# New orders of the engines' tasks in a four-layer decoder stack of 32 elements

## The chip, the cores and the metric

One core of a Trainium2 chip runs the whole program. The metric is the device time of one execution in microseconds (us). A core has five engines that run side by side, each through its own list of instructions in order: TensorE (PE, matmuls), VectorE (DVE), ScalarE (ACT), GpSimd (POOL) and SyncE (SP, which issues the DMAs here). They wait for one another by semaphores.

## What is computed

For each of 32 elements (128 tokens of 256 channels, and a context of the same size) four layers run one after the other. Cut to what matters:

```python
# layer 0: attention of x to the context, 16 heads; only element 0's result is added, to all elements
x = x + att(x, ctx)[0]
# layer 1: a Mamba-2 block, then a cross-attention with 8 heads
zxbcdt = rms(x) @ in_proj_w                  # z, xBC, dt
xBC = silu(conv(xBC)); dt = softplus(dt + dt_bias)
y = scan over tokens of (decay, dt * x, B) with C; y = y + D_skip * x
x = x + rms(y * silu(z)) @ out_proj_w
x = x + softmax(q k / sqrt(dh)) v @ Wo
# layer 2: causal self-attention, attention to the context (16 heads each, keys cut at a
# length counted from nonzero energies), a feed-forward; a layer norm behind each
# layer 3: causal attention to the context, layer norm, feed-forward with gelu, sum
```

## The kernel before

The work of an element is cut into some 80 tasks with names (`Q2`, `conv0`, `quads3`, `scan` ...). A task has a part on each engine that it needs: of `Q2`, PE does a projection, ACT copies it out of PSUM (`QB`), POOL makes a product for the first query. Elements are interleaved: while the Mamba block of element n runs, the cross-attention of n-1, the two attentions of n-2 and the last layer of n-3 run beside it. `l` is the element's lane (0 to 3), `it.iteration` its group of four.

What runs when is not computed on the chip: each engine has a written-out order. `TASKS` gives a place for each task, `PERIOD` 14 is added for each element, `FIRST` moves the tasks of the first eight elements, `LAST` those of the last six, and `SETUP` places what runs once (layer 0 and the loading and preparing of weights). Sorted, this is PE's order. `SHIFT` moves tasks against it for the other engines. The numbers are places to sort by and nothing else; no instruction waits for a time. Each engine's program is then a loop over its order. For the orders the sort is all:

```python
STAND = {(task, n % G, n // G): place_of(task, n) for task in TASKS for n in range(B)} | {(task, 0, 0): at for task, at in SETUP.items()}
PLACE = {key: n for n, key in enumerate(sorted(STAND, key=STAND.get))}
ORDER = dict(PE=list(PLACE))
for engine, shift in SHIFT.items():
    ORDER[engine] = sorted(PLACE, key=lambda key: round(STAND[key] + shift.get(key[0], 0), 5))
```

From PE's order also follow which of the four PSUM banks (`ring0` to `ring3`, in turn) a task's output takes, and the turns of the four score banks. `SPARE` puts some unneeded matmuls (L634) ahead of a few tasks of the first elements, and is not changed.

The tasks that the prediction follows:
- `Y`: PE multiplies the decays with the inputs of the scan (L858). It waits for `M`, which DVE's `decayed` sets (a product at L1401), behind DVE's `scan` (L1397), which waits for the DMA of `spread`, which follows SP's `ld`.
- `pairs`: PE makes C times B (L843) and turns x (L627); DVE takes them out of PSUM (L1385, L1389, L1391). It waits for DVE's `silu` (L1369), which waits for ACT's tanh (L1121) and so for `conv0` and `conv1` (L1358, L1363).
- `z0` on POOL (`gated`, L1577 and L1578): tz = tz + 1, zs = tz * zs, of 128 x 512. DVE's `Y` (L1410, L1412) waits for it.
- `finish2`, `finish3`, `finish4`: DVE adds an attention and takes its moments; POOL makes the root (L1538); `norm2`, `norm3`, `norm5` on DVE normalise in two steps (L1242, which doesn't wait, and L1244, which waits for the root). `fc2` and `norm4` are the same for the feed-forward.
- `e2`, `n2` (and `e3`, `n3`): PE's energies of the first query (L909) and their count (L916); DVE compares (L1447, L1451); POOL drops what is beyond the length (L1598, L1600).
- `quads2` ... `scores2`, `mT2`, `quadsT2`, `exps2`, `values2`, `attT2`, `back2`: one attention; scores and their maxima (DVE, L1261), the maxima turned (`mT2`), scores again, turned (L731), exponentials (ACT), values (L773), turned back.

Of the kernel before, what the change touches and what calls it, by code (L numbers as in the profile page):

```python
# [62 lines left out]
FIRST = dict(
    K1=(0, -4.8807, 1.8851, 0, 0, -0.0386, 0, 0.3068), K2=(0, 0, 0.0587, 0.2116, 0.4008, -0.0391, 0, 0.0921),
    K3=(0.1497, 0, 0.2746, 0, -0.1241, 0.0178, 0.3449, -0.1021), K4=(-0.0075, 0.3177, -0.0519, 0, -0.0792, 0.0205, 0.0602, 0.0747),
    KE2=(0.464, 0.301, -0.1125, 0, 0, -0.0506, 1.7056, 0.2446),
    KE3=(0.429, 0.0232, 0.1398, -0.6705, -1.2307, -0.6524, 0.0653, 0.0008),
    Q1=(0.3016, 0.1916, 0, -0.1316, 0, 0.0424, 0.2126, -0.4399), Q2=(-0.282, 0, 0.1447, -0.6617, -0.4735, 0, 0.3035, 0),
    Q3=(0.1112, 0.2307, -0.091, -0.1748, -0.0394, -0.1697, 0.0827, -0.0097),
    Q4=(-0.5197, 0, -0.0967, 0, 0.2048, 0.129, -0.0027, 0.0008), V1=(-0.0351, -2.4705, 0, -0.0604, -0.2575, 0, 0.0318, -0.2485),  # L70
    V2=(0.0099, 0.212, -0.1011, -0.1647, -0.1633, -0.0391, -0.4613, 0.1597),
    V3=(2.3657, -0.0525, 0.1717, -0.1675, -0.1913, -0.3927, 0.2399, -0.0516),
    V4=(2.082, -0.1366, 0.1643, 0.3402, -0.1665, 0.024, 0.298, 0.0882), Wo=(0.4946, 0, 0.0308, 0, -0.0088, 0.1772, -0.2974, 0),
    Y=(-0.1446, -0.2213, 0, -0.2465, 0, -0.2111, -0.4731, -0.2058), am=(-0.7507, 0, 0.1238, 0.0772, 0.1122, 0.0313, 0.0705, 0),
    attT2=(0.6134, 0.0615, -0.4802, -0.1547, 0.1304, 0, 0.0174, -0.0163),
    attT3=(-0.5502, -0.0973, 0.1565, -0.0641, 0, -0.0386, -0.2287, 0),
    attT4=(-0.4306, 0.1137, 0.1227, -0.4339, -0.0238, 0.0066, 0, -0.0155),
    back2=(-0.3118, -0.5887, -0.1007, 0.1753, 0.4363, 0.188, -0.0778, -0.0163),
# [1619 lines left out]
```

## Time and profile before

| | us |
|---|---|
| time, median of 3 runs (1673.30 to 1677.19) | 1675.93 |
| time of the profiled execution | 1673.93 |
| its span, from the first to the last instruction | 1672.1 |
| PE busy in the span | 1609.6 |
| DVE busy | 1387.7 |
| ACT busy | 1073.6 |
| POOL busy | 494.2 |

The profile is of one execution. Busy times are sums over all stretches, and a busy PE is not PE at its peak, since its ends are modelled. An engine's idle time is put down to what released it. Rows of a timeline merge equal instructions that follow one another (x9), and their time is that of the group from its first start to its last end. L1401 is line 1401 of the kernel; a line inside a helper stands for all tasks that use it. Spans on POOL are rough.

### The profile page before, as it was taken

How to read it: one execution, taken by the hardware profiler on the slowest of the kernel's cores; microseconds unless marked ns; L12 is line 12 of the kernel's file. 1: busy time of each engine (PE TensorE's matmuls, PEld its weight loads, DVE VectorE, ACT ScalarE, POOL GpSimd, SP SyncE). 2: the span in 40 equal slices, each digit the busy share in tenths (PEclk: the TensorE clock that was granted, in tenths of full speed). 3: DMA queues.
4: the chain of work that ended last, by engine and by line, in shares of the span. 5: the costliest groups of instructions: out<-in, count | busy, mean ns of one | idle time of the engine just before them, and what ended most of it. 6: DMA issues, size and time to landing. Idle time of an engine off the chain costs nothing.

```text
span 1672.1 us, 61077 instructions
## 1 busy us (share of the span) xinstructions
PE 1609.6 (96%) x24963; PEld 1383.7 (83%) x24963; DVE 1387.7 (83%) x3587; ACT 1073.6 (64%) x2797; POOL 494.2 (30%) x1256
## 2 busy tenths in 40 slices
PE   7889999999999999999999999999999999999886
PEld 6777888888888888888888888888888888888774
DVE  4588888888888889888888988888898888888552
ACT  2356666766666676666667666666766666676552
POOL 1333223333322332332233233223323322332110
PEclk9999999999999999999999999999999999999997
DMA  6120001000000000000000000000000000000000
GB/s 208 43 81 21 5 19 31 18 25 28 21 2 25 24 25 25 25 22 4 25 24 25 24 24 23 4 24 25 25 24 25 16 10 24 22 28 18 5 5 7
DMA packets 31316, 44.36 MB, mean 27 GB/s; under 512 B 3008, under 2 KB 26176, under 8 KB 30912
## 3 DMA queue, kind: packets, MB, share of 16 engines
q1 hardware_dynamic: 31040, 40.46, 7.6%
q8 instruction: 201, 3.29, 0.8%
q14 instruction: 75, 0.61, 0.1%
HBM read 36.12 MB, written 4.33 MB: 24 GB/s over the span
## 4 chain that ended last, share of the span: by engine, by line
PE 56%; DVE 35%; issue 5%; POOL 2%; DMA 1%; ACT 1%; DVEq 0%; SPq 0%; POOLq 0%; ACTq 0%
PE ring L639 20%; PE ring L645 14%; PE ring L627 6%; DVE conv L1363 5%; DVE maxima_at L1261 5%; PE score L707 4%; DVE decay L1397 3%; PE score L731 3%; PE ring L773 3%; DVE conv L1369 2%; PE ring L858 2%; DVE decay L1401 2%; DVE QB L1272 2%; DVE conv L1358 2%; PE score L671 2%
## 5 line engine op out<-in xcount | busy, mean ns | idle before, releaser
L1538 POOL TENSOR_TENSOR stat<-stat 128x1 f32<-128x1 f32 x224 | 131.7, 594 | 612.8 <-DVE stat L1227 612.3
L1019 ACT COPY actT<-ring 128x256 f32<-128x256 f32 x256 | 95.5, 373 | 264.6 <-PE ring L627 264.2
L1261 DVE TENSOR_REDUCE maxima_at<-score 128x4 f32<-128x512 f32 x388 | 240.8, 684 | 26.0 <-PE score L707 25.2
L1052 ACT ACTIVATE weights<-score 128x512 f32<-128x512 f32 x388 | 200.6, 607 | 28.6 <-PE score L731 28.1
L1363 DVE SCALAR_TENSOR_TENSOR conv<-raw,vectors,conv 128x128 f32<-128x128 f32 x576 | 169.2, 349 | 6.8
L639 PE MATMUL ring<-actT,w_q 128*128 128x128 f32 x1024 | 141.4, 281 | 0.7 <-ACT actT L1019 0.7
L639 PEld LDWEIGHTS ring<-actT,w_q 128*128 128x128 f32 x1024 | 124.5, 191 | 12.8 <-issue 11.3
L639 PE MATMUL ring<-actT,w_up 128*128 128x128 f32 x1024 | 129.1, 280 | 0.5 <-ACT actT L1019 0.5
L639 PEld LDWEIGHTS ring<-actT,w_up 128*128 128x128 f32 x1024 | 120.6, 194 | 3.7 <-ACT actT L1019 1.1
L731 PE MATMUL score<-QB,KE 32*128 32x128 f32 x3104 | 116.7, 286 | 3.8 <-issue 2.8
L1187 ACT ACTIVATE gT<-ring,vectors 128x128 f32<-128x128 f32 x256 | 73.0, 368 | 70.3 <-PE ring L639 69.6
L731 PEld LDWEIGHTS score<-QB,KE 32*128 32x128 f32 x3104 | 97.7, 189 | 23.7 <-issue 19.3
L645 PE MATMUL ring<-w_down,gT 128*128 128x256 f32 x512 | 115.9, 379 | 1.3 <-issue 1.3
L773 PE MATMUL ring<-weights,V 128*32 128x128 f32 x3104 | 106.6, 279 | 3.8 <-issue 3.5
L1070 ACT ACTIVATE KE<-K,const 128x128 f32<-128x128 f32 x256 | 106.3, 503 | 0.0
L645 PEld LDWEIGHTS ring<-w_down,gT 128*128 128x128 f32 x512 | 94.9, 190 | 13.1 <-issue 1.4
L639 PE MATMUL ring<-cT,w_k 128*128 128x128 f32 x768 | 104.4, 279 | 0.0
L1063 ACT COPY attT<-ring 128x512 f32<-128x512 f32 x97 | 56.2, 579 | 72.0 <-PE ring L773 71.9
L773 PEld LDWEIGHTS ring<-weights,V 128*32 128x32 f32 x3104 | 80.4, 111 | 26.1 <-ACT V L1036 11.8
L645 PE MATMUL ring<-w_v,cT 128*128 128x256 f32 x384 | 100.0, 383 | 0.5 <-ACT V L1036 0.5
L639 PE MATMUL ring<-actT,w_in 128*128 128x128 f32 x768 | 98.8, 279 | 1.1 <-DVE q_bias L1342 1.1
L639 PEld LDWEIGHTS ring<-cT,w_k 128*128 128x128 f32 x768 | 95.5, 192 | 4.9 <-issue 0.2
(179 smaller groups left out, 3809.7 us busy)
## 6 DMA issues: line engine op xcount, KB each, us to landing
decay<-rates_out SPq DMA_DIRECT2D x32, 512.0 KB, 4.1
cT<-in_ctxT SPq DMA_DIRECT2D x32, 128.0 KB, 2.2
x_in<-in_x SPq DMA_DIRECT2D x32, 128.0 KB, 2.5
out<-result SPq DMA_DIRECT2D x32, 128.0 KB, 2.1
row_all<-in_rows SPq DMA_DIRECT2D x1, 1420.0 KB, 10.2
w_in<-in_in_proj SPq DMA_DIRECT2D x1, 1288.0 KB, 6.5
w_k<-in_k SPq DMA_DIRECT2D x4, 256.0 KB, 7.4
w_v<-in_v SPq DMA_DIRECT2D x4, 256.0 KB, 7.2
```

The costliest lines, as they stand in the source:

```text
L627: last = nc.tensor.transpose(t[:, c * P:(c + 1) * P], src[:, c * P:(c + 1) * P], ident)
L639: last = mm(t[:, at:at + P], w[:, c, cols:cols + P], xT[:, c, :], start=(c == 0), stop=(c == n - 1))
L645: last = mm(t[:, at:at + hi - lo], xT[:, c, :], w[:, c, lo:hi], start=(c == 0), stop=(c == n - 1))
L731: last = mm(score[:, r, at:at + P], KE[rows_of, l, c, e, :], QB[rows_of, l, c, e, :], start=(not masked and at == 0), stop=(c == DC - 1 an ...
L773: last = mm(output[ROWS_OF[r], four * P:(four + 1) * P], V2[:, l, h, :], weights[:, buffer, h % 8 // 2, at:at + P], start=True, stop=True)
L1019: nc.scalar.copy(dst.rearrange("p c k -> p (c k)"), t[:, 0:n]).then_inc(read, 1)
L1052: run(weights[:, turned_buffer(it, a_, l), r, :], score[:, r, :], ACT.Exp).then_inc(S["exps"], 1)
L1070: last = run(KE[:, l, c, e, :], K2[:, l, c, :], ACT.Identity, scale=own[:, e:e + 1], bias=spare_row[:, 2 * c + e:2 * c + e + 1])
L1187: last = run(gT[:, l % 2, c, :], t[:, k * P:(k + 1) * P], ACT.Gelu, bias=up_b[:, c:c + 1])
L1261: nc.vector.tensor_reduce(maxima_at[:, maxima_buffer(it, a_, l), 32 * r:32 * (r + 1)].rearrange("p (f s) -> p s f", f=2)[:, 0:DC, :], scor ...
L1363: last = stt(conv[:, l % 2, c, :], raw[:, l % 2, c, k:k + P], conv_w[:, c, k:k + 1], conv[:, l % 2, c, :], ALU.mult, ALU.add)
L1538: tt(stat[:, l, 10:11], stat[:, l, 2:3], stat[:, l, 4:5], ALU.pow).then_inc(S[done], 1)
```

## The change

All tables of places get new values: `TASKS`, `FIRST`, `LAST`, `SETUP` and `SHIFT`. Nothing else is changed: the same instructions, with the same operands and the same waits, stand in other orders on PE, ACT, DVE, POOL and SP, and the PSUM banks follow PE's order. The diff, cut (of `FIRST` one entry, of `LAST` none):

```diff
--- before.py
+++ after.py
 TASKS = dict(
-    K1=27.1941, K2=36.4796, K3=45.2686, K4=51.2561, KE2=36.4927, KE3=55.6023, Q1=30.3419, Q2=36.7225, Q3=45.6768, Q4=56.4087,
-    V1=20.4169, V2=38.4481, V3=46.9887, V4=51.4714, Wo=34.4797, Y=25.7148, am=-0.1642, attT2=46.178, attT3=19.8436, attT4=54.723,
-    back2=42.7145, back3=51.1225, back4=64.1374, conv0=15.1721, conv1=-1.5314, ctxT=34.1467, decayed=32.8056, down=71.1144,
-    dt=1.3854, e2=37.8777, e3=47.2433, exps2=47.7111, exps3=10.232, exps4=21.6756, fc1=53.239, fc2=54.3499, finish1=-9.1617,
-    finish2=43.1974, finish3=49.378, finish4=63.2585, ld=21.3616, loadc=21.5812, loadx=-12.121, mT2=40.0837, mT3=48.4859,
-    mT4=58.9877, n2=40.7882, n3=47.7104, norm2=33.7236, norm3=22.9718, norm4=37.5768, norm5=62.8256, pairs=21.8762, proj=26.9634,
-    quads1=31.0824, quads2=38.3064, quads3=46.4563, quads4=57.4583, quadsT2=40.7773, quadsT3=49.6848, quadsT4=61.9224, row=44.5976,
-    scan=14.2492, scores1=32.2004, scores2=32.0011, scores3=47.3368, scores4=68.1586, silu=20.9204, softplus=18.9875,
-    spread=22.7901, store=23.1605, turn1=32.8102, uT=26.5226, up0=66.8312, up1=67.8745, values1=33.4323, values2=42.004,
-    values3=50.5514, values4=63.0522, x1=14.4949, x1r=12.6782, x2T=35.2831, x3T=44.7168, x4T=52.7176, x5T=55.6828, x6T=65.7536,
-    xbc0=16.7051, xbc1=18.0605, xhat=30.6529, xhatT=15.884, xnT=28.5927, z0=20.9215, z1=17.7244)
+    K1=29.0856, K2=38.5366, K3=47.2992, K4=53.4458, KE2=33.3045, KE3=54.7332, Q1=32.1044, Q2=38.6937, Q3=47.6381, Q4=58.0962,
+    V1=22.2425, V2=39.4232, V3=48.7148, V4=53.3289, Wo=36.4551, Y=27.2567, am=-2.2834, attT2=47.4617, attT3=22.0271,
+    attT4=55.3422, back2=44.2681, back3=52.8769, back4=65.9856, conv0=16.6179, conv1=1.221, ctxT=36.0313, decayed=34.6925,
+    down=72.9489, dt=8.0634, e2=41.4217, e3=49.0318, exps2=48.4908, exps3=10.3026, exps4=24.4833, fc1=54.9532, fc2=55.9444,
+    finish1=-9.0188, finish2=44.2731, finish3=52.0631, finish4=64.0237, ld=23.1242, loadc=21.3662, loadx=1.2509, mT2=41.7171,
+    mT3=49.4892, mT4=60.582, n2=42.8035, n3=49.2859, norm2=36.1002, norm3=24.6855, norm4=38.5896, norm5=65.8112, pairs=23.7157,
+    proj=28.8669, quads1=32.8573, quads2=40.0966, quads3=48.2938, quads4=59.6247, quadsT2=42.5242, quadsT3=51.4302,
+    quadsT4=63.7535, row=47.0248, scan=14.9081, scores1=34.1206, scores2=32.7622, scores3=49.3269, scores4=69.5119,
+    silu=22.5319, softplus=20.0592, spread=24.3395, store=17.5935, turn1=34.6091, uT=28.0478, up0=68.7197, up1=69.5352,
+    values1=35.1323, values2=43.7462, values3=52.6753, values4=64.8371, x1=16.1732, x1r=15.149, x2T=37.0825, x3T=47.0926,
+    x4T=54.2481, x5T=57.5334, x6T=67.586, xbc0=18.2029, xbc1=19.9444, xhat=31.9447, xhatT=17.8431, xnT=30.9408, z0=22.2265,
+    z1=19.6646)
...
 FIRST = dict(
...
-    x1=(-5.3355, -6.7716, -12.2611, 0.5214, 0.2413, 0.0991, 0, 0.8625),
+    x1=(-14.0516, -0.9067, -10.7956, -0.0199, -1.0892, -0.1852, 0.6475, -0.2856),
...
 LAST = dict(
...
 SETUP = dict(
-    K0=-87.7724, Q0=-89.7619, V0=-69.5516, attT0=10.1131, back0=-17.5369, bias=-2.2664, exps0=-87.3874, finish0=-14.8614,
-    load_mamba=-134.5546, load_w1=-78.5301, load_w2=-73.1891, load_w3=55.6841, mT0=-27.2745, prep_in=-35.9796, prep_masks=1.0364,
-    prep_out=4.1588, prep_q1=18.1022, quads0=-69.2113, quadsT0=-23.49, scores0=-90.8413, values0=-21.1918)
+    K0=-108.4361, Q0=-316.1758, V0=-86.2378, attT0=-84.2212, back0=-27.465, bias=7.5052, exps0=-101.3015, finish0=-13.4217,
+    load_mamba=-255.8636, load_w1=-177.3492, load_w2=-83.867, load_w3=42.2511, mT0=-76.1239, prep_in=-73.3065,
+    prep_masks=-11.5938, prep_out=-5.107, prep_q1=20.9471, quads0=-80.3574, quadsT0=-63.3098, scores0=-144.0343,
+    values0=-39.3738)
 SHIFT = dict(
     ACT=dict(
-        K2=0.4275, K4=0.371, KE2=2.1051, KE3=-8.3627, Q1=0.2401, Q2=0.4113, Q3=0.0246, Q4=1.2096, V1=0.0661, V2=0.6553, V3=0.3112,
-        Y=1.0681, attT2=-3.4331, attT3=31.0217, attT4=8.7138, ctxT=-0.4571, exps2=-6.4438, exps3=39.9244, exps4=40.2808,
-        fc1=0.7372, ld=-0.1039, row=0.2044, scores1=-0.7902, silu=-0.1882, softplus=-0.2365, turn1=0.1793, uT=0.4762, up0=0.6797,
-        up1=0.4246, x1=-0.5175, x2T=-0.0673, x3T=0.071, x4T=0.2522, x5T=0.318, x6T=0.3578, xbc0=0.1868, xbc1=0.439, xhatT=0.0635,
-        xnT=0.9282, z0=0.0015, z1=0.2322, K0=-24.9607, Q0=-31.7526, V0=-0.7018, attT0=-21.6729, exps0=39.9731, prep_in=-3.1006),
+        K0=2.3774, K2=-0.1878, K4=0.1396, KE2=5.8104, KE3=-5.9146, Q0=-4.9669, Q1=0.0129, Q2=0.1419, Q3=-0.1146, Q4=0.5104,
+        V0=-5.1257, V1=0.0207, V2=0.1395, V3=0.3629, Y=0.4866, attT0=-2.6608, attT2=-4.1728, attT3=30.4973, attT4=9.4546,
+        ctxT=-0.3027, exps0=-0.1648, exps2=-6.1821, exps3=41.2393, exps4=39.4704, fc1=0.0001, ld=-0.2582, prep_in=0.4989,
+        row=-0.2399, scores1=-0.9947, silu=-0.0344, softplus=0.3518, turn1=-0.1135, uT=-0.1483, up0=0.0492, up1=-0.1419,
+        x1=-0.3812, x2T=-0.1308, x3T=-0.1741, x4T=-0.2178, x5T=-0.7925, x6T=0.0128, xbc0=0.0375, xbc1=0.141, xhatT=-0.4344,
+        xnT=-0.0197, z0=0.0624, z1=0.1306),
     DVE=dict(
-        K1=1.0572, K3=0.57, V4=0.4841, Wo=1.1062, Y=0.609, conv0=3.1201, conv1=22.4343, decayed=-7.3402, down=1.5737, e2=0.5677,
-        e3=-0.0785, fc2=0.652, finish1=43.3665, finish2=0.278, finish3=2.0689, finish4=1.3234, mT2=0.6229, mT3=0.8259, mT4=0.5286,
-        n2=0.9079, n3=0.7485, norm2=10.4211, norm3=29.708, norm4=17.8864, norm5=2.0685, pairs=0.2116, proj=0.8909, scan=10.8396,
-        scores1=-0.5025, scores2=7.84, scores3=-0.7238, scores4=-9.0893, silu=1.0136, softplus=0.4775, uT=0.6437, x1=-1.3524,
-        x1r=1.7364, x3T=0.0339, xhat=-15.2978, xnT=0.2024, finish0=3.4964, mT0=-11.4439, prep_in=10.1597, prep_masks=14.7529,
-        prep_out=12.705, prep_q1=-0.1445, scores0=-43.4431),
+        K1=0.737, K3=0.7294, V4=1.0082, Wo=0.4816, Y=0.7142, conv0=3.7868, conv1=21.2406, decayed=-7.2188, down=0.835,
+        e2=0.6758, e3=0.1793, fc2=0.6105, finish0=-0.1091, finish1=44.8348, finish2=0.4507, finish3=2.2334, finish4=1.8583,
+        mT0=-4.1163, mT2=0.6697, mT3=0.4952, mT4=1.0277, n2=0.0766, n3=0.7025, norm2=8.9344, norm3=29.7647, norm4=18.6129,
+        norm5=1.9381, pairs=-0.0496, prep_in=-2.0909, prep_masks=-3.6299, prep_out=23.6362, prep_q1=-1.1374, proj=0.7365,
+        scan=12.0106, scores0=-10.8877, scores1=-0.3252, scores2=8.8541, scores3=-0.2306, scores4=-8.6395, silu=0.6896,
+        softplus=1.2879, uT=0.737, x1=-0.5296, x1r=1.3903, x3T=-0.5879, xhat=-14.8904, xnT=-0.6414),
     POOL=dict(
-        Q2=1.2684, Q3=-0.9315, V4=4.8789, am=21.0272, dt=14.5564, fc2=-0.1102, finish2=0.1706, finish3=3.4551, finish4=2.5198,
-        n2=-0.0248, n3=2.0304, norm5=3.5039, proj=0.6654, softplus=1.1659, uT=-0.0221, x1r=1.4386, z0=1.9558),
+        Q2=-0.6859, Q3=-1.4596, V4=-1.2884, am=21.2566, dt=9.5868, fc2=-2.2711, finish2=0.0217, finish3=-0.2182,
+        finish4=-0.7242, n2=-1.1406, n3=-1.8819, norm5=-0.3809, proj=-0.436, softplus=-1.4643, uT=-1.3189, x1r=0.1378,
+        z0=2.3456),
     SP=dict(
-        ld=8.6234, loadc=-5.0975, loadx=16.7863, spread=13.2176, store=78.055, load_mamba=-31.3063, load_w1=-56.8981,
-        load_w2=2.0842, load_w3=-3.921))
+        ld=6.0333, load_mamba=-7.3208, load_w1=13.4741, load_w2=-9.0565, load_w3=-30.545, loadc=-6.3444, loadx=-5.8078,
+        spread=7.0578, store=60.6588))
```

Sorted, the tables give for one period of the steady part (element +0 is the one whose `xhatT` comes first):

```
POOL before: dt+0 Q3-2 softplus+0 am+0 n3-2 z0+0 finish4-3 Q2-1 norm5-3 finish3-2 fc2-2 uT+0 n2-1 proj+0 x1r+1 V4-2 finish2-1
POOL after:  dt+0 Q3-2 softplus+0 am+0 n3-2 finish4-3 norm5-3 finish3-2 Q2-1 V4-2 z0+0 fc2-2 uT+0 n2-1 proj+0 x1r+1 finish2-1
DVE before:  xhat+0 finish2-2 norm2-2 down-4 x3T-2 scores4-3 mT4-3 scores1-1 K3-2 conv0+0 scores3-2 e3-2 softplus+0 finish1-1 n3-2 conv1+0 mT3-2 Wo-1 silu+0 pairs+0 finish4-3 norm5-3 finish3-2 V4-2 e2-1 norm3-2 scan+0 decayed+0 scores2-1 Y+0 mT2-1 fc2-2 x1+1 uT+0 norm4-2 n2-1 proj+0 K1+0 x1r+1 xnT+0
DVE after:   xhat+0 down-4 x3T-2 scores4-3 mT4-3 scores1-1 K3-2 conv0+0 scores3-2 e3-2 softplus+0 finish1-1 mT3-2 n3-2 conv1+0 Wo-1 silu+0 pairs+0 finish4-3 norm5-3 finish3-2 V4-2 norm3-2 scan+0 decayed+0 scores2-1 Y+0 e2-1 mT2-1 fc2-2 uT+0 n2-1 norm4-2 proj+0 x1+1 K1+0 xnT+0 x1r+1 finish2-1 norm2-1
PE before:   xhatT+0 Q1-1 row-2 xbc0+0 x3T-2 mT4-3 quads1-1 K3-2 Q3-2 z1+0 xbc1+0 quads3-2 turn1-1 V3-2 e3-2 values1-1 n3-2 quadsT4-3 ctxT-1 V1+0 Wo-1 mT3-2 z0+0 values4-3 x2T-1 ld+0 quadsT3-2 pairs+0 back4-3 K2-1 values3-2 Q2-1 back3-2 K4-2 V4-2 x6T-3 e2-1 quads2-1 V2-1 x4T-2 up0-3 fc1-2 Y+0 up1-3 mT2-1 fc2-2 uT+0 quadsT2-1 n2-1 proj+0 K1+0 x5T-2 values2-1 Q4-2 xnT+0 back2-1 down-3 quads4-2
PE after:    xhatT+0 Q1-1 xbc0+0 mT4-3 quads1-1 row-2 x3T-2 K3-2 Q3-2 z1+0 xbc1+0 quads3-2 turn1-1 V3-2 e3-2 values1-1 n3-2 mT3-2 quadsT4-3 ctxT-1 z0+0 V1+0 Wo-1 values4-3 x2T-1 ld+0 quadsT3-2 pairs+0 back4-3 K2-1 values3-2 Q2-1 back3-2 V4-2 V2-1 K4-2 x6T-3 quads2-1 x4T-2 up0-3 fc1-2 Y+0 e2-1 up1-3 mT2-1 fc2-2 uT+0 quadsT2-1 n2-1 proj+0 K1+0 x5T-2 values2-1 Q4-2 back2-1 xnT+0 down-3 quads4-2
SP before:   ld+0 loadc+1 store-5 loadx+2 spread+0
SP after:    ld+0 spread+0 store-3 loadx+3 loadc+2
```

ACT's order changes in the same manner (`z0` ahead of `silu`, `attT4` and `ld` ahead of `x2T`, `KE2` and `V2` ahead of `K4`). At the start, SP's `load_w3` comes ahead of the first `ld`; ACT's `prep_in` comes behind `attT0`, and DVE's `prep_masks` ahead of `finish0`.

## Rows read from the trace of the kernel before

**Rows 1.** The page: busy us (share) of the engines; the last chain's shares

```profile
PE 1609.6 (96%) x24963; PEld 1383.7 (83%) x24963; DVE 1387.7 (83%) x3587; ACT 1073.6 (64%) x2797; POOL 494.2 (30%) x1256
...
PE 56%; DVE 35%; issue 5%; POOL 2%; DMA 1%; ACT 1%; DVEq 0%; SPq 0%; POOLq 0%; ACTq 0%
```

**Rows 2.** Windows: length, busy us (count) PE, PEld, DVE, ACT, POOL, clock, DMA, GB/s

```profile
187.00:1545.00 1358.00, 1346.70 (x21404) 1162.68 (x21403) 1194.60 (x3085) 924.27 (x2417) 424.57 (x1085) 1.00 0.07 21
0.00:187.00 187.00, 161.97 (x2239) 139.64 (x2240) 133.70 (x352) 88.68 (x236) 55.88 (x142) 0.98 0.25 80
1545.00:1672.10 127.10, 100.92 (x1324) 81.41 (x1323) 59.42 (x152) 60.70 (x145) 13.78 (x29) 0.88 0.02 6
```

**Rows 3.** Timeline of PE, Y of two elements: start, us, what [idle before]

```profile
858.43 1.10 PE L858 MATMUL ring<-dbx,decay 128*32 128x64 f32 x64 [0.15 <-DVE decay L1401]
...
907.12 1.10 PE L858 MATMUL ring<-dbx,decay 128*32 128x64 f32 x64 [0.15 <-DVE decay L1401]
```

**Rows 4.** Instructions of L1397, 200 to 1540 us: duration ns min/median/max, starts

```profile
L1397 DVE TENSOR_TENSOR_SCAN decay<-decay,delta x28: 2281/2284/2286, 219.3 to 1538.8; 128x1024 f32<-128x1024 f32 x28
```

**Rows 5.** Timeline of DVE, one element, from pairs to decayed

```profile
846.36 0.29 DVE L1385 TENSOR_TENSOR state_gate<-ring,const 128x128 f32<-128x128 f32 x1 [0.58 <-PE ring L843]
...
853.42 0.41 DVE L1482 TENSOR_TENSOR V<-ring,row_all 128x256 f32<-128x256 f32 x1
...
854.34 0.49 DVE L1244 SCALAR_TENSOR_TENSOR res<-att,stat,row_all 128x256 f32<-128x256 f32 x1
854.74 2.28 DVE L1397 TENSOR_TENSOR_SCAN decay<-decay,delta 128x1024 f32<-128x1024 f32 x1
857.06 1.23 DVE L1401 TENSOR_TENSOR decay<-decay,state_gate 128x1024 f32<-128x1024 f32 x1
```

**Rows 6.** Timeline of POOL, the same element: z0, Q2, root of finish3, V4

```profile
845.81 1.50 POOL L1577 TENSOR_SCALAR tz<-tz 128x512 f32<-128x512 f32 x1
847.39 1.28 POOL L1578 TENSOR_TENSOR zs<-tz,zs 128x512 f32<-128x512 f32 x1
...
851.24 0.28 POOL L1589 TENSOR_TENSOR q_first<-QB,const 128x16 f32<-128x16 f32 x1 [0.39 <-ACT QB L1025]
...
853.68 0.55 POOL L1538 TENSOR_TENSOR stat<-stat 128x1 f32<-128x1 f32 x1 [1.33 <-DVE stat L1227]
...
868.99 0.12 POOL L1604 MEMSET V<- 128x16 f32 x1
```

**Rows 7.** Timeline of POOL at four places where it met DVE

```profile
40.96 1.50 POOL L1577 TENSOR_SCALAR tz<-tz 128x512 f32<-128x512 f32 x1 [2.30 <-ACT tz L1116]
...
76.86 1.51 POOL L1577 TENSOR_SCALAR tz<-tz 128x512 f32<-128x512 f32 x1 [1.45 <-ACT tz L1116]
...
120.36 3.29 POOL L1578 TENSOR_TENSOR zs<-tz,zs 128x512 f32<-128x512 f32 x1
...
600.76 0.62 POOL L1598 TENSOR_TENSOR V<-V,keep 128x256 f32<-128x256 f32 x1 [0.31 <-ACT tz L1116]
```

**Rows 8.** Timeline of DVE at these places, and nine undisturbed products of conv1

```profile
40.71 1.26 DVE L1363 SCALAR_TENSOR_TENSOR conv<-raw,vectors,conv 128x128 f32<-128x128 f32 x3
...
77.34 0.96 DVE L1369 SCALAR_TENSOR_TENSOR conv<-raw,conv 128x768 f32<-128x768 f32 x1 [3.40 <-ACT raw L1121]
...
120.29 2.29 DVE L1397 TENSOR_TENSOR_SCAN decay<-decay,delta 128x1024 f32<-128x1024 f32 x1
...
600.80 1.39 DVE L1369 SCALAR_TENSOR_TENSOR conv<-raw,conv 128x768 f32<-128x768 f32 x1
...
840.18 2.70 DVE L1363 SCALAR_TENSOR_TENSOR conv<-raw,vectors,conv 128x128 f32<-128x128 f32 x9
```

**Rows 9.** Timeline of PE: e2

```profile
706.48 0.31 PE L909 MATMUL ring<-q_first,K 128*32 128x8 f32 x16
```

**Rows 10.** Waits of DVE: us in total, times, longest

```profile
DVE decay L1397 <- DMA decay<-rates_out: 2.1, 1, 2.1
```

**Rows 11.** Timeline of DVE at the start: the second part of prep_in

```profile
22.14 0.17 DVE L1320 TENSOR_SCALAR row_all<-row_all 128x8 f32<-128x8 f32 x1 [1.65 <-ACT row_all L1091]
```

246 lines of the change are left out of this document (128 added, 118 removed).

## The prediction

> **What bounds the kernel now.** I read the busy table and the windows first. TensorE (PE) is busy 96% of the span [rows 1], and in the steady part, 187 to 1545 us, it works 1346.7 of 1358.0 us at full clock; what it loses lies in the head (25 of 187 us idle) and the tail (26 of 127 us) [rows 2]. That reads as "PE-bound", but the chain of work that ended last gives only 56% to PE and 35% to VectorE (DVE) [rows 1], so in the steady part both hand the chain to each other. Where? PE's timeline shows it at task Y: each time PE sat idle 0.15 us there, released by DVE's multiplication at L1401 [rows 3]. Two Y stand 907.12 - 858.43 = 48.69 us apart, the period of an element. The multiplication begins at 857.06 and takes 1.23 us, so it ends at 858.29, and PE starts Y at 858.43, 0.14 later [rows 3, 5]. So task `decayed` on DVE releases Y, and everything that PE does after Y (up to quads3), what DVE does from there to `silu`, and what DVE does from `pairs` to `decayed` is one closed ring. Whatever lengthens one link of the ring lengthens every element by as much; whatever shortens a link that is not in the ring brings nothing.
>
> The link to look at is pairs to decayed on DVE: from the state_gate at 846.36 to 858.29 it works nearly without a gap, with V4 at 853.42, the second half of norm3 at 854.34, the scan at 854.74 and the multiplication at 857.06 [rows 5]. Each of the 28 scans from 219 to 1539 us takes 2281 to 2286 ns: nothing disturbs them before the change [rows 4].
>
> **The change, part by part.** No instruction is added or removed, so only waits and meetings can change.
>
> *Steady part, GpSimd (POOL).* Before, its task z0 (L1577, 1.50 us, and L1578, 1.28 us) ran at 845.81 to 848.67 [rows 6], beside DVE's pairs, which take one operand from PSUM. The change sorts z0 behind finish4, norm5, finish3, Q2 and V4. So it can't start before POOL's root of finish3 is done, 853.68 + 0.55 = 854.23, and then Q2's product (0.28) and V4's memset (0.12) [rows 6]: 854.6. That is on top of norm3's second half, the scan and the multiplication, which run from 854.34 to 858.29 [rows 5] and which read two operands from SBUF, as z0's instructions do one or two.
>
> What such a meeting costs is in the trace at four places. (a) POOL's L1578 began at 120.36, 0.07 after a scan, and took 3.29 us in place of 1.28; it ended at 123.65, 1.07 after the scan's end at 122.58 [rows 7, 8]: POOL stands still while DVE's instruction runs, and goes on as soon as it ends. (b) POOL's two-operand L1598 began at 600.76, 0.04 before DVE's silu: silu took 1.39 us, where another took 0.96; that is 0.43 longer, while POOL's 0.62 is no longer than at other times [rows 7, 8]: DVE stood still until about 0.2 us before POOL's end (600.80 + 0.43 = 601.23 of 601.38). (c) L1577 at 40.96 beside three conv products: these took 1.26 us, where nine take 2.70, so about 0.9: 0.36 longer. (d) L1577 at 76.86 with silu starting 0.48 later: silu took 0.96, nothing lost [rows 7, 8]. So L1577 stops DVE only when it gets in first, and for some 0.36 us; L1578 stops it almost to its end.
>
> Put together in the new order: L1577 asks at 854.6, stands until norm3's second half ends (854.34 + 0.49 = 854.83), and gets in ahead of the scan, which loses 0.35 by (c) and ends at 854.74 + 2.28 + 0.35 = 857.37. L1577 ends at about 856.3; L1578 then stands behind the scan, by (a), gets in at 857.37 and needs 1.07 us, to 858.44. The multiplication would start at 857.4 and stands until 0.2 us before that, by (b): 0.8 us. Sum on the ring: 0.35 + 0.8 = 1.15 us per element, all of it at Y, since PE waits there already. The ends: 0 if DVE keeps its turn throughout (a rival below), and 1.28 + 0.36 = 1.64 if both POOL instructions are paid in their full time; no meeting in the rows makes DVE faster, so there is no end below nothing. I take 1.15: both steps have a row of the same two instructions or the same operands.
>
> The Trainium skill (SBUF — State Buffer, "SBUF: two separate sides") says that DVE and GpSimd share a port pair under an exclusive lock, and that the one that starts first holds it for its whole instruction while the other fully blocks. Rows (a) and (b) agree; row (d) does not for L1577: silu began inside it and lost nothing. By the rule L1577 would hold the scan for its remaining 1.4 us, and the multiplication would still lose about 1: 2.4 us per element; it is the last rival.
>
> *Steady part, PE.* e2 goes from ahead of quads2 to behind Y. Ahead of Y its time was outside the ring (Y waits for DVE anyway), behind it it is inside: at most its 0.31 us [rows 9]. xbc0 and mT4 go ahead of row and x3T, mT3 ahead of quadsT4, z0 ahead of V1 and Wo, V4 and V2 ahead of K4: the same work in other neighbourhoods. mT4 now comes sooner after quads4 and may wait for the maxima; the neighbourhoods may give back as much. I take +0.1 us per element, with ends -0.15 (nothing of e2 seen, and half of it given back) and +0.31.
>
> *Steady part, DVE and ACT.* e2 leaves the stretch ahead of the scan, but norm3's second half waits for POOL's root (854.23) and starts at 854.34 [rows 5, 6], so nothing comes of it. mT3 ahead of conv1 makes the tanh for silu later by about the two instructions of mT3; silu stands behind Wo on DVE anyway, so nothing or a few hundredths. xhat behind norm2 fills the wait for quads4. ACT's moves (z0 ahead of silu, x2T behind attT4 and ld) are one instruction each, with their readers later. All nothing; if a cover is gone, the cost is that one instruction, which the +0.31 above takes in.
>
> *SP queue.* spread follows ld directly, with its DMA: earlier, with slack ahead of the scan. The store of n-3 now stands ahead of loadx and loadc, so their two DMAs wait for down; their readers are two and three elements later: nothing.
>
> *Head and tail.* load_w3 goes ahead of ld.0, and spread.1 no longer stands behind loads: DVE's one wait for that DMA was 2.1 us [rows 10], which I give back. Against it, ACT's prep_in goes behind attT0, and DVE's prep_in waits for it (already 1.65 us before [rows 11]), with prep_masks now ahead of finish0; I give that -1 of gain back as +1, and 2 us of gain for the rest of the 51 us that PE is idle at both ends [rows 2]. Sum -3 us, ends -6 and +2.
>
> **Sum.** 28 elements [rows 4] x (1.15 + 0.1) = 35.0; less 3 is +32. The profiled execution's time is 1673.9 us (span 1672.1), 2.0 below the median of 1675.9; to the median the forecast is 1675.9 + 32 = 1708 us.
>
> **The rivals.**
> 1. *Lighter meeting.* The scan starts ahead of L1577, which gets in only at the scan's end; the multiplication pays 0.35 by (c), and L1578 stands behind it. For it: the scan's start at 854.74 lies ahead of norm3's end at 854.83. Against: conv's products in (c) followed each other as closely. 28 x (0.35 + 0.1) - 3 = +10: 1686.
> 2. *Faster: the port is never lost to POOL.* DVE's instructions follow so closely from 854.34 to 858.29 that POOL gets in at no boundary; z0 runs after 858.29 and ends near 861.1, when DVE's L1410, the first to want it, comes up behind scores2. It decides at the boundary at 854.83. Then the ring pays nothing, PE's neighbourhoods decide: at -0.15 and an end gain of 4, 28 x -0.15 - 4 = -8: 1668. For it: 28 undisturbed scans, though none met z0. Against: (a).
> 3. *As in 2, but PE at +0.1*: 28 x 0.1 - 3 = 0: 1676, no change to be measured.
> 4. *Whole-instruction hold*, 2.4 us per element: 28 x 2.5 - 3 = +67: 1743. Row (d) speaks against it.
>
> **How the numbers follow.** Forecast 0.42, rival 1 0.18, rival 2 0.24, rival 3 0.12, rival 4 0.04. About 0.2% (3.4 us) is what a measurement of this kernel can tell from no change. Faster 0.24, same 0.12, slower 0.64. The forecast's own range, with 0.9 to 1.5 us per element and the ends, is 1695 to 1720. To hold 8 in 10 the range takes in rivals 1 and 3 and half of rival 2: 1668 to 1716.
>
> **What would show it.** Right: scans at L1397 of 2.6 us in place of 2.28 and multiplications at L1401 of about 2.0 in place of 1.23, POOL's L1578 longer than 1.28, still 0.15 us from L1401's end to Y, and Y 49.9 us apart. Rival 1: scans unchanged, L1401 at 1.6. Wrong altogether: both unchanged and Y 48.5 to 48.8 apart; or another wait than L1401 ahead of Y, which would mean that the ring is closed elsewhere.

## The result and the profile after

The changed kernel is slower: 1718.73 us, median of 4 runs (1716.82 to 1720.94), against 1674.62 for the kernel before, timed beside it; ratio 1.0272, 95% interval 1.0234 to 1.0311. The forecast was 1708 with a range of 1668 to 1716; the time lies 2.7 us above the range. The profiled execution took 1716.82 us (span 1715.0), 42.9 more than that of before. The page of after, busy times and last chain, as [rows 1]:

```profile
PE 1601.8 (93%) x24963; PEld 1382.3 (81%) x24963; DVE 1424.5 (83%) x3587; ACT 1079.1 (63%) x2797; POOL 507.0 (30%) x1256
...
PE 67%; DVE 20%; ACT 6%; issue 3%; POOL 2%; DMA 1%; SPq 0%; DVEq 0%; POOLq 0%; ACTq 0%
```

DVE is busy 36.8 us longer with the same instructions, PE 7.8 us less. And ACT, 1% of the last chain before, now has 6%. The first was expected; the second was not. (Lines stand 14 lower in the file after: L1397 is L1411 now, L1401 is L1415, L1577 is L1591.)

Where is the time? From Y of element 3 to Y of element 31, the windows of before, then of after (columns as in [rows 2]):

```profile
174.37:1542.47 1368.10, 1356.80 (x21533) 1171.43 (x21533) 1202.66 (x3109) 933.13 (x2440) 427.71 (x1092) 1.00 0.07 21
```

```profile
171.94:1586.75 1414.81, 1354.05 (x21532) 1172.59 (x21533) 1237.76 (x3109) 938.09 (x2441) 444.63 (x1092) 1.00 0.07 20
```

These 28 elements take 46.7 us more; the start is 2.4 shorter (171.9 for 174.4 us), the end 1.4 (128.3 for 129.7). PE works as long as before at the same clock, so the 46.7 us are idle time of PE. Its timeline of after, one element, answers [rows 3]:

```profile
879.53 1.10 PE L872 MATMUL ring<-dbx,decay 128*32 128x64 f32 x64 [1.61 <-DVE decay L1415]
...
909.14 0.30 PE L641 MATMUL ring<-const,maxima_at 128*128 128x128 f32 x1 [0.83 <-ACT V L1050]
...
930.27 1.10 PE L872 MATMUL ring<-dbx,decay 128*32 128x64 f32 x64 [1.60 <-DVE decay L1415]
```

Two Y stand 930.27 - 879.53 = 50.74 us apart, 2.05 more than in [rows 3]. PE is idle 1.6 us ahead of Y where it was 0.15, and 0.83 us in a place where it never was: ahead of L641, which is `mT3`, released by ACT's L1050, the copy of `V3` out of PSUM.

The first wait is the meeting. Instructions of the scan and of the multiplication, answering [rows 4] (ns, least, median, most):

```profile
L1411 DVE TENSOR_TENSOR_SCAN decay<-decay,delta x28: 2303/2697/2700, 217.0 to 1581.8; 128x1024 f32<-128x1024 f32 x28
```

```profile
L1415 DVE TENSOR_TENSOR decay<-decay,state_gate x28: 1448/2110/2116, 219.7 to 1584.5; 128x1024 f32<-128x1024 f32 x28
```

One meeting in the timelines of POOL and DVE:

```profile
873.49 0.55 POOL L1552 TENSOR_TENSOR stat<-stat 128x1 f32<-128x1 f32 x1 [1.33 <-DVE stat L1241]
...
874.24 1.75 POOL L1591 TENSOR_SCALAR tz<-tz 128x512 f32<-128x512 f32 x1
876.08 2.23 POOL L1592 TENSOR_TENSOR zs<-tz,zs 128x512 f32<-128x512 f32 x1
```

```profile
874.14 0.48 DVE L1258 SCALAR_TENSOR_TENSOR res<-att,stat,row_all 128x256 f32<-128x256 f32 x1
874.54 2.70 DVE L1411 TENSOR_TENSOR_SCAN decay<-decay,delta 128x1024 f32<-128x1024 f32 x1
877.27 2.11 DVE L1415 TENSOR_TENSOR decay<-decay,state_gate 128x1024 f32<-128x1024 f32 x1
```

The scan takes 0.41 us longer than in [rows 4], the multiplication 0.88 longer than the 1.23 of [rows 5]: together 1.30 us. POOL's L1592 ends at 878.31, 1.07 behind the scan's end (877.24), as in place (a) of the prediction; the multiplication stands 0.88 us, to 878.15, 0.16 before that end, as in (b).

The second wait, in the timeline of ACT ahead of PE's `mT3` at 909.14:

```profile
906.03 1.07 ACT L1071 COPY weights<-ring 128x512 f32<-128x512 f32 x2 [0.72 <-PE ring L641]
906.99 1.65 ACT L1084 ACTIVATE KE<-K,const 128x128 f32<-128x128 f32 x4
908.54 0.46 ACT L1050 ACTIVATE V<-ring,mask 128x256 f32<-128x256 f32 x1
```

`mT3` doesn't read V3. But the tasks with an output in the ring take its four PSUM banks in turn, in PE's order, and that is now V3, e3, values1, n3, mT3: `mT3` gets V3's bank, and ACT empties that only behind `KE3`, four instructions of 1.65 us in all. Before, ctxT, V1 and Wo stood between n3 and mT3, so that mT3 took n3's bank, and PE didn't wait for it in the middle.

### The profile page after: what moved, and what is told of

Its sections match the earlier page's. It is cut to its first block, busy times and chain, and to the rows that moved or that the text cites. A ratio compares the mean times of both kernels' runs of the same rounds, so it can differ in the third digit from the quotient of the medians.

```text
span 1715.0 us, 61181 instructions
## 1 busy us (share of the span) xinstructions
PE 1601.8 (93%) x24963; PEld 1382.3 (81%) x24963; DVE 1424.5 (83%) x3587; ACT 1079.1 (63%) x2797; POOL 507.0 (30%) x1256
## 4 chain that ended last, share of the span: by engine, by line
PE 67%; DVE 20%; ACT 6%; issue 3%; POOL 2%; DMA 1%; SPq 0%; DVEq 0%; POOLq 0%; ACTq 0%
PE ring L659 18%; PE ring L653 18%; PE ring L641 9%; PE score L745 6%; PE ring L787 4%; DVE decay L1411 4%; PE score L721 4%; DVE decay L1415 3%; ACT KE L1084 2%; PE score L685 2%; POOL stat L1552 2%; PE ring L872 2%; ACT weights L1071 2%; DVE bn L1245 1%; DVE att L1295 1%
## 5 line engine op out<-in xcount | busy, mean ns | idle before, releaser
L1286 DVE SCALAR_TENSOR_TENSOR QB<-ring,const,QB 128x256 f32<-128x256 f32 x194 | 84.6, 477 | 25.5 <-PE ring L641 25.3
L1258 DVE SCALAR_TENSOR_TENSOR res<-att,stat,row_all 128x256 f32<-128x256 f32 x128 | 63.0, 492 | 40.9 <-POOL stat L1552 34.4
```

The lines of the kernel that those rows point to most:

```text
L1286: last = stt(QB[:, l, :, e, :], t[:, 0:P].unsqueeze(1).broadcast_to((P, DC, P)), either_row[:, e:e + 1], QB[:, l, :, e, :], ALU.mult, ALU.add)
```

## The experiments

So the theory is: two prices, 1.30 us of meeting and the wait ahead of `mT3`. Its rivals: all of it is the meeting (PE would wait at Y for what it doesn't wait at mT3); all of it is PE's order. The runs stood beside the kernel before on other chips, where that took 1670 to 1671 us, so times are compared by ratios to it (1.0272 for the changed kernel); the times in the expectations are those of the first chip, where before took 1674.62. The pitch, the distance of two Y, is read from PE's timeline in the middle (elements 10 to 26), as most elements there have it. The diffs are cut to the numbers that change.

**1. z0 early again, on POOL alone.**

```diff
 POOL=dict(
-        z0=2.3456),
+        z0=-1.6),
```

> The changed kernel with one number put back: GpSimd's z0 stands behind n3 and ahead of finish4 again, as before the change. Theory (two prices on the ring: z0's meeting with the scan and the multiplication, 0.41 + 0.89 = 1.30 us an element, and TensorE's wait of 0.84 us ahead of mT3): scans are 2.28 us and multiplications 1.23 again, TensorE's wait ahead of Y falls from 1.6 to about 0.3 us, the wait ahead of mT3 stays at 0.84, two Y stand about 49.45 us apart in place of 50.74: 1718.7 - 28 x 1.30 = 1682 us. Rival A (the meeting is the whole loss, and the wait ahead of mT3 lies in time that TensorE would wait at Y anyway): two Y 48.7 apart, about 1671 us. Rival B (the loss is TensorE's new order, the meeting lies in slack): time unchanged, 1719.

Measured: 1698.19 us, ratio 1.0169 (1.0154 to 1.0184) where 1682 us is 1.004; pitch 49.79 us in most elements, 49.45 in five. Scans 2.28, multiplications 1.23 us, the wait ahead of mT3 still 0.82. So the meeting is gone and the second price stays, as the theory has it, but only 0.95 us of 1.30 came back. The rest is a new meeting, POOL and DVE:

```profile
809.68 1.51 POOL L1591 TENSOR_SCALAR tz<-tz 128x512 f32<-128x512 f32 x1
```

```profile
809.75 1.35 DVE L1383 SCALAR_TENSOR_TENSOR conv<-raw,conv 128x768 f32<-128x768 f32 x1 [0.28 <-ACT raw L1135]
```

z0 got in 0.07 us ahead of `silu`, which took 1.35 us in place of the 0.96 of [rows 8], and `pairs` waits for silu (PE idle 0.28 there). In the five elements with a pitch of 49.45, silu got in first: POOL's L1591 began 0.22 to 0.98 us behind its start and took up to 2.14 us, and DVE lost at most 0.04. There the whole price is back (50.74 - 49.45 = 1.29 us).

**2. V3 ahead of KE3, on ACT alone.**

```diff
 ACT=dict(
-        V3=0.3629
+        V3=0.0
```

> The changed kernel with one number changed: in ScalarE's order V3's copy out of PSUM goes ahead of KE3 (four instructions, 1.65 us), behind turn1. TensorE's order and its PSUM banks stay. Theory (TensorE waits ahead of mT3 because mT3's output goes to the bank that V3 still fills, four uses back, and ScalarE empties it only behind KE3): the wait ahead of mT3 goes from 0.84 to 0; of it come off the ring between 0.35 us (then silu on VectorE is the last for pairs) and 0.84 us: 28 x 0.35 to 28 x 0.84 off 1718.7, that is 1695 to 1709 us, scans and multiplications still 2.70 and 2.11 us. Rival A (the meeting on VectorE is the whole loss): time 1719, TensorE waits 2.4 us ahead of Y in place of 1.6. Rival C (mT3 waits for the maxima from VectorE, not for the bank): the wait ahead of mT3 stays.

Measured: 1709.35 us, ratio 1.0243 (1.0226 to 1.026), pitch 50.04. PE's waits from 500 to 1450 us, first after, then with the edit (us in total, times, longest):

```profile
PE ring L872 <- DVE decay L1415: 27.4, 17, 1.7
PE ring L641 <- ACT V L1050: 15.7, 19, 0.8
```

```profile
PE ring L872 <- DVE decay L1415: 29.5, 18, 1.7
...
PE ring L641 <- ACT V L1050: 0.8, 1, 0.8
```

The wait ahead of mT3 is gone by an edit that touches neither PE's order nor mT3's operand: it was the bank, and not DVE's maxima. Of 0.83 us, 0.70 came off the pitch (0.61 as the mean of elements 10 to 26); PE waits 0.07 longer at Y and now and then at pairs for a part of the rest. The meeting is as it was (scans 2.70, multiplications 2.11). The time gained less than expected: 1695 to 1709 us are ratios of 1.012 to 1.021, and the interval overlaps that of the changed kernel, so by the time alone this price isn't shown. In the trace Y of element 3 to Y of element 31 takes 1402.9 us in place of 1414.8, 11.9 less; in the first and last few elements the pitch is nearly that of the changed kernel.

**3. Both.** The two edits above.

> Both edits together: z0 on GpSimd behind n3, V3 ahead of KE3 on ScalarE. Theory: both prices come off, 28 x (1.30 + 0.35 to 0.84) = 46 to 60 us off 1718.7, but no less than TensorE's own work of some 48.4 us an element allows: two Y 48.6 to 49.1 apart, 1669 to 1673 us, about 2 to 5 us below the kernel before, since start and end are 3.9 us shorter than before. Rival A: the same as z0 alone. A third price in the new order (e2 behind Y, ScalarE's z0 ahead of silu) would leave two Y more than 49.1 apart.

Measured: 1681.96 us, ratio 1.0074 (1.0056 to 1.0091). In the middle the pitch is 48.73 us, 2.01 less than after and 0.04 more than before: there the two prices are nearly all of it (the meeting with silu is gone there too: z0 begins 0.98 us behind silu's start, and 8.9 us ahead of the scan as it did before). The time missed the expected 1669 to 1673 (a ratio below 1). From Y of element 3 to Y of element 31 it is 6.7 us longer than before. In elements 3, 4, 7 and 26, which `FIRST` and `LAST` move, the single number didn't bring V3 ahead of KE3, and the waits of 0.8 to 0.9 us stayed; without them (experiment 10) the stretch is 2.9 us shorter. In five of the outer elements (4, 7, 9, 28, 31) z0 still met silu, which took 1.18 to 1.35 us.

**4. z0 late on the kernel before, with Q2 and V4 as in the new order.**

```diff
 POOL=dict(
-        Q2=1.2684, V4=4.8789, z0=1.9558
+        Q2=2.23, V4=1.6, z0=4.68
```

> The kernel before with GpSimd's order alone changed to the new one: z0 behind finish4, norm5, finish3, Q2 and V4. Theory: scans 2.70 and multiplications 2.11 us, 1.30 us an element: 1674.6 + 28 x 1.30 = 1711 us, two Y 50.0 apart, no new wait ahead of mT3. Rival A (the meeting is the whole loss): 1721 us, two Y 50.7 apart. Rival B (the meeting lies in slack): 1675 us.

Measured: 1745.0 us, ratio 1.0451 (1.0432 to 1.0469), pitch 51.17 us: twice as much as expected, by something else. PE's waits, 500 to 1450 us:

```profile
PE ring L909 <- POOL q_first L1589: 34.8, 18, 2.0
```

L909 is e2, which stands ahead of quads2 there and needs POOL's product for Q2, and that now stands behind the root of finish3. DVE's e2 and all that is behind it come later:

```profile
889.21 0.17 DVE L1447 TENSOR_SCALAR nonzero<-ring 128x16 bf16<-128x16 f32 x1 [1.30 <-PE ring L909]
...
890.21 3.36 DVE L1397 TENSOR_TENSOR_SCAN decay<-decay,delta 128x1024 f32<-128x1024 f32 x1
```

So the move of e2 behind Y, which I costed as a small loss, is what covers POOL's Q2 in its new place: the changed kernel, with the same place for Q2, doesn't wait ahead of e2. The scan of 3.36 us is a third form of the meeting: z0 began 1.71 us ahead of it, and L1578 was in first.

**5. The same with Q2 where it was.**

```diff
 POOL=dict(
-        V4=4.8789, z0=1.9558
+        V4=1.6, z0=4.68
```

> The kernel before with z0 and V4 alone moved on GpSimd, z0 behind finish3 and V4; Q2 stays ahead of norm5 (with Q2 moved too, TensorE waited 1.88 us ahead of e2, which here stands ahead of quads2 and needs Q2's product). Theory: no wait ahead of e2; z0 asks at the root's end as in the changed kernel: scans 2.70, multiplications 2.11 us, 1.30 us an element, two Y 50.0 apart, 28 x 1.30 = 36 us slower than before. Rival E (the 1.88 us ahead of e2 came from z0 itself): the wait ahead of e2 stays, two Y 51.2 apart.

Measured: 1707.05 us, ratio 1.0226 (1.0203 to 1.0249), pitch 49.91 in the middle: the meeting alone costs 1.22 us an element on the kernel before, 36 us in all, as expected. The size came out as expected, the place only by half: z0 asks 0.81 us ahead of the scan here and meets the second half of norm3 in place of the scan (0.81 us for 0.48; DVE):

```profile
871.97 0.81 DVE L1244 SCALAR_TENSOR_TENSOR res<-att,stat,row_all 128x256 f32<-128x256 f32 x1
872.70 2.28 DVE L1397 TENSOR_TENSOR_SCAN decay<-decay,delta 128x1024 f32<-128x1024 f32 x1
875.01 2.11 DVE L1401 TENSOR_TENSOR decay<-decay,state_gate 128x1024 f32<-128x1024 f32 x1
```

**6. More work for POOL, so that it comes too late.** In two of 28 elements of the changed kernel POOL has `norm5` between finish3 and Q2 (`FIRST`), and z0 comes 0.18 us behind the scan's start. POOL and DVE there:

```profile
319.11 3.43 POOL L1591 TENSOR_SCALAR tz<-tz 128x512 f32<-128x512 f32 x1
```

```profile
318.92 2.30 DVE L1411 TENSOR_TENSOR_SCAN decay<-decay,delta 128x1024 f32<-128x1024 f32 x1
321.26 1.45 DVE L1415 TENSOR_TENSOR decay<-decay,state_gate 128x1024 f32<-128x1024 f32 x1
```

That is rival 1 of the prediction. Two memsets more bring it about in all elements:

```diff
                     evacuated(it, "V4", l)
+                    for again in range(2):
+                        step(nc.gpsimd.memset(V2[:, l, :, DH16], 1.0))
                     nc.gpsimd.memset(V2[:, l, :, DH16], 1.0).then_inc(S["V4ones"], 1)
```

> The changed kernel with two more memsets on GpSimd ahead of V4's own (the same ones written again, each ended before the next): only work is added, and z0 asks some 0.4 us later. Theory (who gets in first decides the price: in elements 6 and 9 of the changed kernel z0 began 0.18 us behind the scan's start in place of 0.30 ahead of it, the scan took 2.30, the multiplication 1.45 us): 0.24 us an element in place of 1.30, two Y 49.7 apart in place of 50.74, 28 x 1.06 = 30 us faster than the changed kernel, some 1685 to 1690, with 31 instructions doubled or more. Rival D (GpSimd's and VectorE's instructions share the same time whoever is first): as slow as the changed kernel, or slower by the added work.

Measured: 1692.96 us, ratio 1.0134 (1.0113 to 1.0155), pitch 49.67: some 1.3% faster than the changed kernel, by added work. POOL, then DVE, of one element:

```profile
916.00 3.35 POOL L1591 TENSOR_SCALAR tz<-tz 128x512 f32<-128x512 f32 x1
919.43 1.28 POOL L1592 TENSOR_TENSOR zs<-tz,zs 128x512 f32<-128x512 f32 x1
```

```profile
915.76 2.29 DVE L1411 TENSOR_TENSOR_SCAN decay<-decay,delta 128x1024 f32<-128x1024 f32 x1
918.08 1.45 DVE L1415 TENSOR_TENSOR decay<-decay,state_gate 128x1024 f32<-128x1024 f32 x1
```

POOL pays (3.35 us for 1.50) and DVE loses 0.22 us. Who gets in first decides, and not how much the two have to do. The pitch came as expected, the time gained less than the expected 30 us: the ratio fell from 1.0272 to 1.0134, some 23 us, and Y of element 3 to Y of element 31 takes 1388.9 us for 1414.8, 25.9 less. Two elements had been light already, which is 2 of the missing 4 us; the rest wasn't followed.

**7. mT3 early on the kernel before, on PE alone.**

```diff
 TASKS = dict(
-    mT3=48.4859
+    mT3=47.85
 DVE=dict(
-        mT3=0.8259
+        mT3=1.4618
```

> The kernel before with TensorE's mT3 alone in its new place, behind n3 and ahead of quadsT4 (VectorE's order stays). Theory (its output bank is V3's, four uses back, which ScalarE empties only behind KE3, in the old order too): TensorE waits about 0.8 us ahead of mT3 in nearly every element, and since before the change pairs waits for nothing that is later than TensorE, most of it comes on the ring: 0.7 us an element, as the V3 edit took off, two Y 49.4 apart in place of 48.7, 28 x 0.7 = 20 us slower, ratio 1.012. Rival (VectorE's silu is the last for pairs here, and hides it): two Y 48.7 to 48.9 apart, ratio 1.000 to 1.003. Rival C (mT3 waits for VectorE's maxima): a wait of another size, released by VectorE.

Measured: 1722.62 us, ratio 1.0304 (1.0286 to 1.0321), pitch 50.23: 1.54 us an element and not 0.7. PE's waits, 500 to 1450 us:

```profile
PE ring L627 <- ACT V L1036: 15.4, 19, 0.8
PE ring L645 <- DVE QB L1272: 12.4, 18, 1.0
```

The first is the expected one, 0.81 us. The second, 0.66 us ahead of z0 in most elements, is the same once more: from mT3's new place z0 is four uses on (mT3, ctxT, V1, Wo, z0), so it takes mT3's bank, which DVE empties behind conv1. The new order doesn't pay that: there z0 stands ahead of V1 and Wo and takes the bank of values1, Wo takes mT3's, and DVE has mT3 ahead of conv1. Which of these moves would be enough was not tested; I had them all at nothing.

**8. The two mended from element 3 on, V3 always ahead of KE3.**

```diff
+    if engine == "POOL":
+        ORDER[engine] = sorted(PLACE, key=lambda key: round(STAND[key] + (-1.6 if key[0] == "z0" and G * key[2] + key[1] >= 3 else shift.get(key[0], 0)), 5))
+    if engine == "ACT":
+        for l, i in [(n % G, n // G) for n in range(B)]:
+            order = ORDER[engine]
+            if order.index(("V3", l, i)) > order.index(("KE3", l, i)):
+                order.remove(("V3", l, i))
+                order.insert(order.index(("KE3", l, i)), ("V3", l, i))
```

> The changed kernel with GpSimd's z0 early from element 3 on (for elements 0 to 2 it stays late: with z0 early there, Y of element 3 came 5.2 us later in the trace of the z0 edit alone) and ScalarE's V3 directly ahead of KE3 in all elements (the numbers that had moved it left a wait of 0.8 us ahead of mT3 in elements 3, 4, 7 and 26). Theory (the two prices are all of the loss; start and end are 3.9 us shorter than before): Y of element 3 near 172 us, two Y 48.7 us apart in the middle, 28 x 48.9 = 1369 to Y of element 31, 128 us behind it: 1668 to 1672 us for a kernel before of 1672, ratio 0.997 to 1.000. Rival (a third price in the new order, as e2 behind Y or ScalarE's z0 ahead of silu, or in the tables of the first and last elements): ratio 1.003 or more, and the place is seen as TensorE's idle time ahead of one task.

Measured: 1688.22 us, ratio 1.0103 (1.0085 to 1.0121), slower than with the two numbers of experiment 3, where 0.997 to 1.000 was expected. For elements 5 and 29 KE3 stands ahead of the next element's turn1 on ACT; with V3 put ahead of both, ACT stood still for V3, and PE's values1 (L772 there) waited behind it:

```profile
PE ring L772 <- ACT weights L1079: 7.3, 3, 3.6
```

The four waits ahead of mT3 that experiment 3 had left are gone.

**9. The same with e2 back ahead of quads2 for elements 8 to 24** (on PE and DVE; POOL's Q2 ahead of norm5 for these).

```diff
+    if task == "e2" and 8 <= n < 25:
+        moved = -1.70
```

> As the kernel with both edits from element 3 on, and for elements 8 to 24 also e2 on TensorE ahead of quads2 and on VectorE ahead of norm3, as before the change, with GpSimd's Q2 ahead of norm5 for these. Theory (e2 behind Y costs TensorE's 0.14 us that the chain of the changed kernel shows for it, since it lies on the ring there): two Y 0.14 us closer for these 17 elements, 48.6 in place of 48.73, 2.4 us less in all. Rival (it costs nothing, or e2 waits for GpSimd's product): two Y as far apart, or further.

Measured: 1697.1 us, ratio 1.0157 (1.0136 to 1.0178); the pitch is 49.38 for these elements, 0.65 more, where the theory had 0.14 less. PE, then DVE's waits (500 to 1450 us):

```profile
863.81 0.31 PE L933 MATMUL ring<-q_first,K 128*32 128x8 f32 x16 [0.42 <-DVE V L1506]
```

```profile
DVE nonzero L1471 <- PE ring L933: 10.6, 16, 1.0
```

With V4 and V2 ahead of K4, e2 in its old place is four uses behind V4 and waits for DVE to empty that bank; then DVE waits 0.66 us for e2, and norm3 and the scan stand behind it. So the price of e2 behind Y by itself was not measured.

**10. As 8, but V3 moved only where KE3 stands behind turn1.**

```diff
+            turn = ("turn1", (l + 1) % G, i + (l + 1) // G)
+            if turn in PLACE and order.index(turn) < order.index(("KE3", l, i)) < order.index(("V3", l, i)):
```

> The changed kernel with z0 early from element 3 on and V3 ahead of KE3, but only where KE3 stands behind the next element's turn1 on ScalarE (with V3 forced ahead of it for elements 5 and 29 too, ScalarE stood still and TensorE's values1 waited 3.6 and 3.1 us). Theory (with the two prices gone nothing of the new order costs more than 0.1 us an element): Y of element 3 to Y of element 31 in 1381.8 - 6.7 = 1375 us or less, against 1368.1 of the kernel before, ratio 1.000 to 1.006, no gain over the kernel before that can be measured. Rival (the new order is worth something once its two faults are mended): ratio 0.997 or less.

Measured: 1676.05 us, ratio 1.0033 (1.002 to 1.0045); Y of element 3 to Y of element 31 in 1371.9 us, 3.8 more than before, pitch 48.73. Mended in two places, the new order is close to the old one, 0.3% slower, and no version beat the kernel before.

## Why the prediction was right and wrong

**The ring and the meeting: right.** Y follows the multiplication by 0.15 us in the middle, as before, and what lengthens scan or multiplication lengthens the element. The meeting came where it was put and with its two terms: L1591 cost the scan 0.41 (0.35 forecast), L1592 the multiplication 0.88 (0.8 forecast), 1.30 in place of 1.15. On the kernel before, the meeting costs 36 us by experiment 5. The Trainium skill (SBUF — State Buffer, "SBUF: two separate sides") has the one that starts first hold the port pair for its whole instruction. The two-input L1592 did so to within 0.16 us; the one-input L1591 held the scan for 0.41 of its 1.75 us. The rule as written would have given 2.4 us (rival 4); no meeting in these runs cost that.

**Two readings that were inexact.** "L1577 stops DVE only when it gets in first" is not what row (d) shows: L1577 was in first there, by 0.48 us, and silu lost nothing. What counts is how far into L1577 DVE asks (the last section). And "no meeting in the rows makes DVE faster, so there is no end below nothing" overlooked that a new order can also end a meeting. In 28 of the 29 elements from 3 on of the kernel before, silu overlaps n3's L1598 and takes 1.09 us or more in place of 0.96; POOL, then DVE:

```profile
844.35 0.62 POOL L1598 TENSOR_TENSOR V<-V,keep 128x256 f32<-128x256 f32 x1
```

```profile
844.68 1.10 DVE L1369 SCALAR_TENSOR_TENSOR conv<-raw,conv 128x768 f32<-128x768 f32 x1
```

In the changed kernel silu takes 0.95 to 1.00 us. What these 0.14 us are worth on the ring was not tested.

**Rivals 1 to 3.** Rival 1 is a state of the same kernel: it held in 2 of 28 elements, and experiment 6 brought it about in all by making z0 later. Its point of decision was named rightly: whether the scan or L1577 is first. Rivals 2 and 3, with DVE never losing its turn, held in no element from 3 on.

**The step that failed: "Steady part, PE".** I took the moves on PE as "the same work in other neighbourhoods", with +0.1 us an element and ends of -0.15 and +0.31, made from e2's own duration alone. The change's own section says that the PSUM banks follow PE's order, and I priced operands only, never banks. mT3's bank cost 0.83 us of PE and 0.70 of the pitch by experiment 2, more than twice the upper end of +0.31. I had suspected mT4 of waiting for its maxima; it was mT3, for a bank. What else the new orders do comes to little in sum: with both prices gone the pitch is 0.04 us above that of before. What gains and losses stand behind these 0.04 us was not taken apart.

**Moves costed at nothing.** "DVE and ACT: all nothing" was right for the whole (the 0.04 us above). But moves hang together: e2 behind Y, booked as a loss, hides POOL's Q2 (experiment 4: 34.8 us of waits in 18 elements), and mT3 moved on PE without the moves around it costs another 0.66 us ahead of z0 (experiment 7). I named no such cover, and no cost without it.

**The sum.** 35.0 us were forecast for 28 elements, 46.7 came. In the middle each pays 2.05 = 1.30 + 0.70 and 0.05 of other things; in the first and last elements the new tables pay less, and the mean is 46.7 / 28 = 1.67. So in the middle the meeting was put 0.15 us too low and PE's part 0.65 too low.

**Head and tail.** Forecast -3, in the two traces -2.4 - 1.4 = -3.8. Both details came as put: DVE's wait for the spread DMA [rows 10] fell from 2.1 to 0.3 us, the wait of prep_in [rows 11] grew from 1.65 to 2.7. But one profile doesn't carry the sum: in experiments 8 and 9, whose orders are the same up to element 8, Y of element 3 came at 178.44 and 171.84 us. Against a spread of 6.6 us, that -3.8 came out near -3 may be luck, and what the start brings stays open.

**The range** ended 2.7 us too low. The forecast's own went to 1720; I cut it at 1716 to hold the rivals below, and had no rival with a wait of PE on top of the meeting.

## What to carry to other kernels

Where buffers are taken in turn by the order of the work, a moved task inherits the buffer of the task so many uses ahead of it: go through the new order, pair each task with the one whose bank it takes, and ask which engine empties that and what stands ahead of it there. Count each move of a reordering as a possible cover of another, and test them one at a time only with their partners. Where two engines share a port, look at who asks first at each boundary, to a tenth of a microsecond: the same two instructions cost nothing or 1.3 us.

## What the runs showed of the hardware

The price of one meeting by the start of z0 against the scan's start (negative: z0 begins ahead of the scan), all measured with the same instructions:

| z0 against the scan | what is longer on DVE | us |
|---|---|---|
| -8.9 (before, and the middle of experiments 3 and 10) | nothing | 0 |
| -10.4, 0.07 ahead of silu (1) | silu 1.35 for 0.96 | 0.39 |
| -1.71 (4) | scan 3.36 | 1.07 |
| -0.81 (5) | norm3's half 0.81, multiplication 2.11 | 1.2 |
| -0.30 (after) | scan 2.70, multiplication 2.11 | 1.30 |
| +0.23 (6) | multiplication 1.45 | 0.22 |

Unexpected was how little of L1577's 1.50 us stops DVE. Experiment 1 has silu at different distances behind its start; POOL and DVE of two elements:

```profile
212.70 1.51 POOL L1591 TENSOR_SCALAR tz<-tz 128x512 f32<-128x512 f32 x1
...
1505.30 1.51 POOL L1591 TENSOR_SCALAR tz<-tz 128x512 f32<-128x512 f32 x1
```

```profile
212.87 1.25 DVE L1383 SCALAR_TENSOR_TENSOR conv<-raw,conv 128x768 f32<-128x768 f32 x1
...
1505.78 0.96 DVE L1383 SCALAR_TENSOR_TENSOR conv<-raw,conv 128x768 f32<-128x768 f32 x1
```

Beginning 0.07 us behind it, silu is 0.39 us longer; 0.17 behind, 0.29; 0.24 behind, 0.22; 0.48 or more behind, not at all. Distance and loss add up to 0.46 or 0.47 us wherever silu begins behind L1591 and loses by it: it goes on 0.46 us after L1591's start. The scan of the changed kernel fits: L1591 stood 0.25 us for norm3's half (1.75 us for 1.50), and the scan, 0.30 us behind its start, lost 0.41, which is 0.46 us after the 0.25. Norm3's half in experiment 5, 0.08 us behind, lost 0.33: some 0.41 in all. L1578 stops DVE for all but its last 0.15 us or so (0.16 in the changed kernel). And two memsets more on POOL, by which z0 began 0.23 us behind the scan's start in place of 0.30 ahead of it, took 1.3% off the time of the kernel.
